# Feed-forward stage: the hidden activation rotated channel-major, its rounding spread over two loop bodies

## The reference

```python
def act_quant(x):
    scale = 127.0 / jnp.clip(jnp.max(jnp.abs(x), axis=-1, keepdims=True), EPS)
    q = jnp.clip(jnp.round(x * scale), -128.0, 127.0) / scale
    return x + jax.lax.stop_gradient(q - x)
def h_bitlinear(x, w):
    xq = act_quant(fwht(x))          # rotate along the channels, then round to 8 bits per token
    wq = weight_quant(w)             # three values
    return jnp.einsum('bsh,oh->bso', xq, wq)
gate = h_bitlinear(hidden_states, w_gate)      # 512 -> 2048
up = h_bitlinear(hidden_states, w_up)
return h_bitlinear(jax.nn.silu(gate) * up, w_down)   # 2048 -> 512
```

## Time and profile before

| | us |
|---|---|
| median of three runs | 3121.78 (3118.45 to 3122.65) |
| profiled execution, its own time | 3120.97 |
| its span in the trace | 3119.2 |
| busy in the span: TensorE, VectorE, ScalarE, GpSimd | 2773.0, 1992.1, 1437.7, 1008.6 |
| feed-forward phase, first transposes of x to the end of the span | 2456.7 to 3119.2 |
| DMA, mean over the span | 93 GB/s |

### The profile page before, as it was taken

The page is one execution under the profiler, slowest core; times in us unless marked ns, Lnnn a source line. Parts: engine busy times, 40 slices in busy tenths (PEclk is TensorE's granted clock), DMA queues, the critical chain, the costliest instruction groups (busy, mean ns, idle before and its releaser), DMA issues. The chain is left out here.

```text
span 3119.2 us, 66716 instructions
## 1 busy us (share of the span) xinstructions
PE 2773.0 (89%) x26968; PEld 1468.7 (47%) x26968; DVE 1992.1 (64%) x2991; ACT 1437.7 (46%) x2378; POOL 1008.6 (32%) x713
## 2 busy tenths in 40 slices
PE   6999999686888888988747999999999799999997
PEld 2444444252453444544424444444444366666664
DVE  3444444459989889898892444445552377777776
ACT  2222222484776767757613322222222256666664
POOL 0000000116527438255390000000000077777776
PEclk9999999887988988989866999999999899999999
DMA  6999889400000000000121022322210111111110
GB/s 239 336 332 334 300 305 313 145 15 1 2 29 2 29 29 2 29 10 21 62 107 42 26 96 81 108 95 95 73 64 27 62 35 40 40 40 40 40 44 31
DMA packets 126284, 290.20 MB, mean 93 GB/s; under 512 B 30480, under 2 KB 35216, under 8 KB 121968
## 3 DMA queue, kind: packets, MB, share of 16 engines
q1 hardware_dynamic: 122608, 261.85, 24.1%
q10 hardware_dynamic: 3456, 25.17, 2.4%
HBM read 244.96 MB, written 42.01 MB: 92 GB/s over the span
## 5 line engine op out<-in xcount | busy, mean ns | idle before, releaser
L2123 POOL TENSOR_TENSOR d_zb<-d_za 128x1024 f32<-128x1024 f32 x32 | 75.3, 2354 | 987.6 <-DVE d_za L2185 987.6
L899 PE MATMUL b_e<-b_hT,s_region 128*128 128x512 f16 x1152 | 283.1, 392 | 47.4 <-DVE s_region L1327 36.5
L1629 PE MATMUL c_r<-c_hT,c_g_pair 128*128 128x512 f16 x1056 | 255.7, 394 | 13.1 <-DVE c_hT L1792 13.1
L1803 DVE SCALAR_TENSOR_TENSOR c_av<-c_r,c_sg 128x512 f32<-128x512 f32 x88 | 60.9, 692 | 301.6 <-PE c_r L1629 241.3
L1990 PE MATMUL d_m<-s_region,d_xiT 128*128 128x512 bf16 x1024 | 237.7, 383 | 6.5 <-ACT d_sg L2075 2.0
L1629 PE MATMUL c_r<-c_hT,c_u_pair 128*128 128x512 f16 x1056 | 243.0, 380 | 0.0
L1629 PE MATMUL c_d<-c_d_pair,c_aT 128*128 128x512 f16 x1056 | 241.0, 379 | 0.0
L1327 DVE SCALAR_TENSOR_TENSOR s_region<-b_e,b_cw,s_region 128x496 f32<-128x496 f32 (+2 forms) x288 | 203.1, 716 | 18.2 <-ACT s_region L1117 9.8
L851 POOL TENSOR_TENSOR b_tmp<-b_L,s_hn 128x496 f32<-128x496 f32 (+30 forms) x124 | 122.6, 988 | 262.0 <-ACT b_L L1100 252.6
L851 POOL TENSOR_TENSOR b_tmp<-b_L,b_U 128x496 f32<-128x496 f32 (+30 forms) x124 | 130.7, 1054 | 223.8 <-ACT b_L L1100 214.4
L899 PEld LDWEIGHTS b_e<-b_hT,s_region 128*128 128x128 f16 x1152 | 103.9, 99 | 188.4 <-DVE s_region L1327 44.2
(11 more groups left out here) (255 smaller groups left out, 6033.0 us busy)
## 6 DMA issues: line engine op xcount, KB each, us to landing
a_cT<-in_ctxT SPq DMA_DIRECT2D x128, 512.0 KB, 9.7
a_cn<-in_ctx SPq DMA_DIRECT2D x128, 512.0 KB, 9.0
a_x_ln<-in_x SPq DMA_DIRECT2D x8, 1024.0 KB, 15.9
a_cw<-in_ctx SPq DMA_DIRECT2D x128, 64.0 KB, 9.6
a_x_res<-in_x SPq DMA_DIRECT2D x32, 256.0 KB, 11.5
x<-a_x_out SPq DMA_DIRECT2D x32, 256.0 KB, 11.3
b_xg<-x SPq DMA_DIRECT2D x8, 1024.0 KB, 5.5
om<-b_hT SPq DMA_DIRECT2D x32, 256.0 KB, 2.0
```

Of the source, the lines that this page charges most:

```text
L899: mm = pe.matmul(p[:], w_qkv[:, a, i, n, c * P:(c + 1) * P], hp[:, b, n, :], start=(n + a + b == 0), stop=(n == DC - 1 and a == 1))
L1629: mm = pe.matmul(out, x, y, start=start and i == 0, stop=stop and i == 2)
L1803: V.scalar_tensor_tensor(av[:], p[:], AS / (WS * HS), sg[:, f % 2, :], ALU.mult, ALU.mult)\
L2123: nc.gpsimd.tensor_tensor(o[:, :, 0, :], a[:, :, 0, :], a[:, :, 1, :], ALU.add).then_inc(bf, 1)
```

## The change

z is now channel-major: partitions are channels within a chunk of 128, the free dimension holds 16 chunks of 128 tokens. For this `rotate_y` takes the Hadamard matrix as the stationary operand and 512 columns of yT as the moving one. The largest magnitude of a token now lies across partitions: VectorE reduces z over the 16 chunks to `zm` (128x128, `largest`, an input with a stride of 128 elements), TensorE transposes it after piece 2 of the gates, VectorE reduces again and makes the factor, ScalarE writes it on a diagonal (`diag`), TensorE multiplies by ones after the gates, which spreads the factors over all partitions, and VectorE scales z with them (`scaled`, two products of 128x1024). ScalarE adds the rounding constant (`whole_z`) in the same body and subtracts it in the next body (`narrow_z`), which gives ziT directly, without transposes and without the clip at 127. The down product belongs to tile k-3 and stands after the transposes of x; the last sum follows in the same body. On VectorE `round_x` stands before `low_xT`; on ScalarE xs stands before the copies of yT. GpSimd's last level waits for the new scaling.

```diff
-        RQ = Ring(st, ["zi0", "zi1", "down", "pad"], 2, "q")
+        RQ = Ring(st, ["largest", "factor", "down", "pad"], 2, "q")
...
                     mm = pe.transpose(p[:, c * P:(c + 1) * P], xq[:, c * P:(c + 1) * P], ident16[:])
                 mm.then_inc(full, 1)
 
-            def gates(i, r):
-                RX.used(pe, r - 1, "xiT")
-                for j in range(NB):
+            def gates(i, r, js):
+                if js[0] == 0:
+                    RX.used(pe, r - 1, "xiT")
+                for j in js:
                     for n, w in (("g", w_g), ("u", w_u)):
                         p, full = RM.open(pe, i, f"{n}{j}")
                         for c in range(DC):
...
                 for j in js:
                     p, full = RM.open(pe, i, f"z{j}")
                     RM.used(pe, i, f"yT{j}")
...
+                    pe.matmul(p[:], had1, yT[:, 4 * j:4 * j + 4, :].rearrange("p c n -> p (c n)"),
+                              start=True, stop=True).then_inc(full, 1)
+
+            def turn_largest(i, r):
+                p, full = RQ.open(pe, r, "largest")
+                pe.wait_ge(zm_ready, i + 1)
+                pe.transpose(p[:, 0:P], zm[:], ident[:]).then_inc(full, 1)
+
+            def spread_factor(i, r):
+                p, full = RQ.open(pe, r, "factor")
+                pe.wait_ge(diag_ready, i + 1)
+                pe.matmul(p[:, 0:P], ones[:], diag[:], start=True, stop=True).then_inc(full, 1)
+
+            def down(i, r):
+                p, full = RQ.open(pe, r, "down")
                 for c in range(WC):
                     if c % (WC // 2) == 0:
-                        RQ.used(pe, i, f"zi{c // (WC // 2)}")
+                        pe.wait_ge(zi_ready, 2 * i + c // (WC // 2) + 1)
                     mm = pe.matmul(p[:], ziT[:, c, :], w_d[:, c, :], start=(c == 0), stop=(c == WC - 1))
                 mm.then_inc(full, 1)
-                RQ.skip(pe, i, "pad")
 
             def body(k, do):
                 r = k + 2
                 if do["main"]:
-                    gates(k, r)
+                    gates(k, r, (0, 1, 2))
+                if do["end"]:
+                    turn_largest(k - 2, r)
+                else:
+                    RQ.skip(pe, r, "largest")
+                if do["main"]:
+                    gates(k, r, (3,))
+                if do["end"]:
+                    spread_factor(k - 2, r)
+                else:
+                    RQ.skip(pe, r, "factor")
                 if do["one"]:
                     rotate_x(k + 1, r)
                 else:
...
                     transpose_x(k + 2, r)
                 else:
                     RX.skip(pe, r, "xT")
+                if do["sum"]:
+                    down(k - 3, r)
+                else:
+                    RQ.skip(pe, r, "down")
+                RQ.skip(pe, r, "pad")
                 if do["main"]:
                     transpose_y(k)
-                if do["end"]:
-                    transpose_zi(k - 2, 0)
-                if do["main"]:
                     rotate_y(k, (0, 1))
...
                 if do["one"]:
...
                 RX.skip(pe, r, "pad")
-                if do["end"]:
-                    down(k - 2)
+                if do["main"]:
+                    rotate_y(k, (2, 3))
 
             steps(pe, body)
 
...
             A = nc.scalar
             act.wait_ge(set_ready, 1)
 
+            def whole_z(i, h):
+                act.wait_ge(zs_ready, 2 * i + h + 1)
+                half = slice(h * W // 2, (h + 1) * W // 2)
+                A.activation(zs[:, half], zs[:, half], ACT.Identity, bias=offset[:, 0:1]).then_inc(whole, 1)
+
+            def narrow_z(i, h):
+                half = slice(h * W // 2, (h + 1) * W // 2)
+                act.wait_ge(whole, 2 * i + h + 1)
+                if h == 0 and not (isinstance(i, int) and i == 0):
+                    RQ.take(act, i + 4, "down")
+                part = ziT[:, WC // 2 * h:WC // 2 * (h + 1), :]
+                A.activation(part.rearrange("p c n -> p (c n)"), zs[:, half], ACT.Identity, bias=offset[:, 1:2])\
+                    .then_inc(zi_ready, 1)
+
             def body(k, do):
                 r, i = k + 2, k - 2
...
                 for j in range(NB):
...
                         A.activation(sg[:, j % 2, :], p[:], ACT.Silu, scale=gsc[:, 0:1]).then_inc(free, 1)
...
+                    if do["sum"] and j < 2:
+                        narrow_z(k - 3, j)
+                    if do["end"] and j == 2:
+                        act.wait_ge(q2, i + 1)
+                        A.activation(diag[:], ident[:], ACT.Copy, scale=fac2[:, 0:1]).then_inc(diag_ready, 1)
+                if do["end"]:
+                    whole_z(i, 0)
                 if do["two"]:
                     p, _ = RX.take(act, r, "xT")
                     RX.take(act, r, "had")
                     A.activation(xT[:, 0, :], p[:], ACT.Copy, scale=HS).then_inc(xT_hi, 1)
+                if do["one"]:
+                    act.wait_ge(q1, 3 * (k + 2))
+                    p, free = RX.take(act, r, "had")
+                    A.activation(xs[:], p[:], ACT.Identity, scale=fac1[:, 0:1], bias=offset[:, 0:1]).then_inc(free, 1)
+                if do["end"]:
+                    whole_z(i, 1)
+
+                def odd(h):
+                    p, free = RM.take(act, k, f"z{2 * h + 1}")
+                    act.wait_ge(first, 4 * k)
+                    A.copy(zo[:, h, :], p[:]).then_inc(free, 1)
+
                 if do["main"]:
                     for j in range(NB):
                         p, free = RM.take(act, k, f"yT{j}")
                         A.copy(yT[:, 4 * j:4 * j + 4, :].rearrange("p c n -> p (c n)"), p[:]).then_inc(free, 1)
...
+                    odd(0)
                 if do["one"]:
                     p, free = RX.take(act, r, "xiT")
                     A.copy(xiT[:].rearrange("p c n -> p (c n)"), p[:].bitcast(BF16)[:, 0:D]).then_inc(free, 1)
+                if do["main"]:
+                    odd(1)
 
             steps(act, body)
 
...
                     if l == 1:
                         pass
                     if l == 2:
-                        pool.wait_ge(zs_ready, NB * i)
-                        pool.wait_ge(am2, 3 * i)
+                        pool.wait_ge(zs_ready, 2 * i)
                     a = src[:].rearrange("p (m two h) -> p m two h", two=2, h=hh)
                     o = dst[:].rearrange("p (m two h) -> p m two h", two=2, h=hh)
                     nc.gpsimd.tensor_tensor(o[:, :, 0, :], a[:, :, 0, :], a[:, :, 1, :], ALU.add).then_inc(bf, 1)
...
                 dve.wait_ge(xT_hi, i + 1)
                 V.scalar_tensor_tensor(xT[:, 1, :], p[:], HS, xT[:, 0, :], ALU.mult, ALU.subtract).then_inc(free, 1)
 
...
+            def scaled(i, r):
+                dve.wait_ge(zi_ready, 2 * i)
+                p, free = RQ.take(dve, r, "factor")
+                for h in range(2):
+                    half = slice(h * W // 2, (h + 1) * W // 2)
+                    ins = V.tensor_tensor(zs[:, half].rearrange("p (c n) -> p c n", n=P),
+                                          z[:, half].rearrange("p (c n) -> p c n", n=P),
+                                          p[:, 0:P].unsqueeze(1).to_broadcast([P, WC // 2, P]), ALU.mult)
+                    ins.then_inc(zs_ready, 1)
+                dve.wait_ge(zs_ready, 2 * i + 2)
+                dve.sem_inc(free, 1)
 
...
-            def sums(i):
+            def sums(i, r):
                 dve.wait_ge(xr_ready, 16 * (i + 1))
                 dve.wait_ge(stored, 16 * i)
-                p, free = RQ.take(dve, i, "down")
+                p, free = RQ.take(dve, r, "down")
+                dve.wait_ge(dsc_ready, i + 1)
                 V.scalar_tensor_tensor(x_out[:], p[:], dsc[:, 0:1], x_res[:], ALU.mult, ALU.add).then_inc(summed, 1)
                 dve.wait_ge(summed, i + 1)
                 dve.sem_inc(free, 1)
 
-            def scale_z(i):
+            def largest(i):
                 dve.wait_ge(bf, 6 * (i + 1))
-                V.tensor_reduce(amax2[:], z[:], AXX, ALU.max, apply_absolute_value=True).then_inc(am2, 1)
+                V.tensor_reduce(zm[:], z[:].rearrange("p (c n) -> p n c", n=P), AXX, ALU.max,
+                                apply_absolute_value=True).then_inc(zm_ready, 1)
+
+            def factor(i, r):
+                p, free = RQ.take(dve, r, "largest")
+                V.tensor_reduce(amax2[:], p[:, 0:P], AXX, ALU.max).then_inc(am2, 1)
                 dve.wait_ge(am2, 3 * i + 1)
+                dve.sem_inc(free, 1)
                 V.tensor_scalar(step2[:, 0:1], amax2[:], W ** -0.5, QEPS, ALU.mult, ALU.max).then_inc(am2, 1)
                 dve.wait_ge(am2, 3 * i + 2)
                 V.reciprocal(inv2[:], step2[:]).then_inc(am2, 1)
                 dve.wait_ge(am2, 3 * i + 3)
+                if not (isinstance(i, int) and i == 0):
+                    dve.wait_ge(diag_ready, i)
```

(49 more changed lines are left out.)

36 lines of the change are left out of this document (4 added, 32 removed).

## The result

The changed kernel takes 3232.8 us, median of 4 runs (3229.01 to 3238.37), against 3122.22 for the kernel before, also 4 runs: a ratio of 1.0356, interval 1.0335 to 1.0377. That is 110.6 us slower; the forecast was 96 slower.

The account below looks back on a forecast made before the run. TensorE was taken as the bound, a loop over VectorE and ScalarE right behind. With 22.6 us bodies, 29 x 3.16 gives +92; with the ends +95.7 on 3120.97, 3216.7, adjusted to 3218 us; range 3160 to 3240.

Parts of the forecast that it names:

- The case that was forecast: Whole kernel: bodies lengthen from 19.44 to 22.6 us, time 3218 us, own range 3200 to 3236; chance 0.60.
- The strided reduction: VectorE's reduction of z at a stride of 128 elements: 3.66 us instead of 2.29, high end 4.17.
- The ring: Fourth stage's loop: one turn of waits between ScalarE, VectorE and TensorE sets the body, 22.6 us instead of 19.44.
- that path 0.65 behind: TensorE's own work before the rotation of y: yT copies come 0.65 us after the transposes of y.
- TensorE stays the bound: Rival for the loop: only the present 0.45 us idles, body 18.64, time 3101 us; chance 0.06.
- is covered enough: Rival of no change: cover leaves idle time of just 1.25 us per body, some 3120 us; chance 0.03.
- Its cover is gone: Down product, moved to mid-body, no longer lies over first-level sums and reduction; TensorE idles 0.64 and 2.45 us there.
- its idle 0.45 us: Kernel before: TensorE's weight load waits for VectorE's y, about 0.45 us real idle time per body.
- `xq` meets GpSimd: VectorE's xq clip meets GpSimd's third level: may last 2.4 us instead of 0.43, still ahead of its transpose.
- The clock: Granted clock expected at 1.00; rival with clock 0.9 adds 19 us, time 3237; chance 0.06.
- The end: From the last reduction to the span's end: 16.0 us before, 19.2 after, +3.2.
- The sum: Whole kernel: bodies 2 to 30 +92, end +3.2, bodies 31 and 32 +1.5, first four -1; +95.7 us.

Follow-up runs that it names:

- the in-order run: Changed kernel with the reduction to zm reading z in order instead of at a stride of 128 elements (wrong maxima); 3180.21 us, 1.0176 to the kernel before.
- the filled kernel: Changed kernel plus eight products that nothing reads, just before the up product of piece 2; 3221.49 us, 1.0308 to the kernel before.

## Why the prediction was right, and where it was off

The case that was forecast is the one that came, and the time lies in its own range of 3200 to 3236; 110.6 us came for 96.

- **The strided reduction**, taken at 3.66 between 2.29 and 4.17: 3.718. Choosing ScalarE's strided pace in place of its extra time was right, and the in-order run shows that this one term is worth 1.5 to 1.7 us of the 3.5 per body. The Trainium skill, Vector Engine (DVE) Microarchitecture Reference, section 5.2 (Measured stream behaviour on trn2), has 1.73 ns per column where single elements of one source hop by 4 KiB, by estimate 3.7 us here; the trace agrees, with 3.718 at hops of 512 bytes, and its other case, a hopping read at full rate, did not come.
- **The ring.** 22.6 forecast, 22.68 in the bodies at full clock. Two runs move single links by known amounts. With the reduction in order the body follows in full, 1.43 for 1.46 at full clock; with the second `whole_z` last it follows by 0.40 of 1.04, until TensorE's own path is the longer one. The forecast had that path 0.65 behind. The rivals in which TensorE stays the bound, or is covered enough, are out: in the first of the two bodies above its records show it idle for 0.23 + 2.12 + 0.85 + 0.16 = 3.36, and with some 0.2 of hand-over that a group's record includes before each of the four, 4.2 (forecast 4.39). What was saved on its work was not on the ring. Each of the new operations cost about what was forecast: scaling 1.217 (1.23), diag 0.402 (0.38), `whole_z` 1.144 (1.10), eight f32 instructions of the rotation at 0.43.
- **"Its cover is gone"** was a right count but a poor reason. Putting the cover back made it 75 us slower. What costs is the length of the turn, 22.6 against 18.2 of TensorE's work; where TensorE idles in it is a matter of order.
- **The kernel before.** The forecast read its idle 0.45 us as a wait for the reduction, the first Silu and the first `y`, with TensorE as the bound. One run moved just this wait to the next piece, another took it off the gates, and both gained nothing; a turn over GpSimd, the second clip and the rounding of x is as long as the body. This did not hurt the forecast, since the changed kernel has no such clip of z and its own ring is 3.2 longer.
- **`xq` meets GpSimd**: 2.4 forecast, 2.457 measured, and hidden, as said.
- **The clock** was the mis-sized term: expected at 1.00, with its fall as a case of 0.06 that took 19 us. It fell in 17 of the 29 bodies, to 0.93 in their mean. In the second of the two bodies above, after an idle time of 2.13 before the up product, four products take 1.89 instead of 1.04:
```profile
2815.11 1.89 PE L1992 MATMUL d_m<-s_region,d_xiT 128*128 128x512 bf16 x4 [2.13 <-DVEq L2207]
```
  That is the lower of the clock's two levels, 1.2 GHz for 2.4. Those products are on the ring, by way of `y` 2 and the factor. Mean body 22.93 less 22.68 is 0.25, 7 us over 29 bodies; the filled kernel gives 11 back, 7.4 of them here. The stretch in the earlier trace rows, with more idle time than this one at a clock of 1.00, did not carry over: the idle share doesn't tell, and both runs that put work into the longest idle time restored the clock. The forecast treated its case and the clock's as alternatives; they added up.
- **The end**, +3.2 forecast (the terms that it lists add up to 18.9 and not 19.2, so +2.9), +8.0 measured. The step summed one down product. There is one `ziT` buffer, so `narrow_z` of the last tile waits until the down product of the tile before is through, and both run one behind the other, slowly:
```profile
3219.20 6.29 PE L2026 MATMUL d_q<-s_region,d_ziT 128*128 128x512 bf16 x16
...
3225.59 2.19 ACT L2085 ACTIVATE d_ziT<-d_zs,d_offset 128x1024 bf16<-128x1024 f32 x2 [2.74 <-PE d_q L2026]
...
3227.90 5.30 PE L2026 MATMUL d_q<-s_region,d_ziT 128*128 128x512 bf16 x16 [2.40 <-ACT d_ziT L2085]
```
  In the earlier trace rows only one of 5.03 lies behind the last reduction. The second one also starts behind the second half of ziT, 1.04 later than the step had it behind the first; the trace names ScalarE's pass as what it waits for, and not why. And about 3 of the 8 are the clock, 0.57 and 0.68 during these two products: in the filled kernel, with the same work behind the last reduction, they are shorter and the end lasts 20.77 instead of 23.93.
- **The sum** by stretches is 101.3 + 1.3 - 1.6 + 8.0 = 109.0, against 110.6 between the medians; the later start of the profiled execution isn't in it. Of the 101.3, 29 x 3.24 = 94 are the ring at full clock (forecast 92) and 7 the clock.

What stays open: why the clock falls in some bodies and not in others with the same idle times.

## What to carry to other kernels

Before moving work off the engine that is 99% busy, add up the turn of waits that runs beside it, link by link; if the turn is longer than what will be left of the work, the turn is the new time, and every operation made slower on it (here a strided read, 1.4 us) counts in full. And a body in which TensorE hardly idles can still have another turn of just its length, here over GpSimd. A long idle time of TensorE costs twice where a product of the ring follows right behind it at a lower clock. At the end of a pipelined loop, count what the single buffers force into a row.

## What the runs showed of the hardware that was not expected

- VectorE's clip from f32 to bf16 of 1024 elements takes 0.69 us with GpSimd idle, and otherwise, in nearly every record, ends about 0.55 us after the GpSimd instruction that was running when it began (2.55, 2.26, 1.85 us, by where it starts); the one of 512 elements 0.28 after (2.43 for 0.43). Reductions and `y` don't do this: the strided reduction takes 3.72 beside GpSimd and 3.58 in the last body, without it. So a small shift of VectorE against GpSimd can cost 2 us per body: at full clock 1.43 became 2.84 in one run, and a second clip that began 1.2 later cost 2.3 in another.
- Eight products that nothing reads made the kernel 11 us faster, through the granted clock.
- Moving one wait of 0.56 us off TensorE in the kernel before gained nothing twice; a turn that runs past TensorE is as long as the body there (ratios 0.9993 and 1.0004).
